# Wider multiplications on VectorE: spectra in six blocks, and three pairs of small instructions merged

## The chip, the cores and the metric

The kernel runs on one core of a Trainium2 chip. The metric is the device time of one launch in microseconds, the median of several runs. The engines of the core are TensorE (matrix products), VectorE and GpSimd (elementwise work), ScalarE (activations and copies) and SyncE, whose queue issues all DMA transfers here.

## The reference, cut to what matters

```python
def _autocorrelation(Q, K, V):              # here K = V = ctx, 8 x 512 x 2048, 8 heads
    qf = jnp.fft.fft(q, axis=2)
    kf = jnp.fft.fft(k, axis=2)
    corr = jnp.fft.ifft(qf * jnp.conj(kf), axis=2).real
    topk = int(C * np.log(L))               # 12 lags for L = 512
    w, idx = jax.lax.top_k(corr.transpose(0, 1, 3, 2), topk)
    w = jax.nn.softmax(w, axis=-1)
    out = jnp.zeros_like(v)
    for i in range(topk):                   # v shifted by each lag, clamped at the last position
        g = jnp.minimum(idx[:, :, None, :, i] + pos, L - 1)
        out = out + w[:, :, None, :, i] * jnp.take_along_axis(v, g, axis=2)
...
x = x + _autocorrelation(_layernorm(x), ctx, ctx)
out = einsum('bsd,od->bso', h, W) + bias     # h = _layernorm(x)
upd = einsum('ebsr,eor,e->bso', einsum('bsd,erd->ebsr', h, A), Bf, coeffs * scales)
x = x + out + upd
```

Each channel of x is correlated over the 512 positions with the same channel of the context. The 12 largest lags get softmax weights, and the context is summed at these shifts. A dense layer with a low-rank update follows.

## The kernel before

The batch (8) and the channels (2048, in chunks of 256) give N = 64 chunks. The program walks through 78 windows. Window w takes chunk w through the correlation and the choice of lags, chunk w - 1 through the weighted sum of shifts, and chunks w + 1 and w + 2 through preparation. From window 14 on it also holds one eighth of the dense layer's product for one half of a group of 512 output columns, so that a batch takes eight windows. Windows 1 to 9 prepare the dense weights (`p_w`, `p_hi`, `p_lo`). Rows of a finished batch (`a_rows`) get the attention added by GpSimd (`add_row`), in four windows of each eight.

All transforms are matrix products. A 512-point transform is folded into four parts of 128 frequencies. TensorE leaves a spectrum of a chunk in PSUM as two pairs of blocks, `ps[:, 2]` and `ps[:, 3]`, each 2 x 256 columns. ScalarE moves the two spectra of the context, `vk` (of the values) and `uk` (of the upper half), to SBUF (`move_spectrum`). A product of two spectra needs each PSUM pair twice, with different blocks of the moved spectrum, and a sum or difference of the results on GpSimd.

VectorE works in a fixed order in each window: `scale_group` (dense output), `multiply_queries` (4 products of 512 columns, into `prod` and `term`, which is the buffer `tf`), `multiply_upper` (4, into `zu` and `tu`), statistics, `multiply_lower` (8, into `zv`, `zf`, `tw`, `tf`), `row_low`, then for the new correlation `part_corr`, `largest`, `choose`, `weights_low`, then `row_statistics`, `part_output` and `row_gain`. `largest` finds the eight largest lags of each of the two halves g of a chunk and negates the maximum; ScalarE takes the exponentials (`exponents`, into `wts`), `choose` removes the chosen lags, sums the kept exponentials into `total`, scales it by a constant and takes the reciprocal `share`.

GpSimd's order in a window is `add_products`, `add_group` (dense output), `add_upper`, `add_lower`, `add_row`, `fold_queries`, `fold_values`, `add_bias`. TensorE's order is `upper_lags` and `lower_lags` of chunk w - 1 (from the transposed weights `w_lag`), `correlate`, `values` and `upper` of chunk w + 1, `output` of chunk w - 1, `queries` of chunk w + 1, with eight pieces of the dense product between them. SyncE's queue is in order too: in a window with a row addition it waits for it, stores the sum (`store_x1`) and loads the next attention rows before it issues the two transposes of the weights (`turn_weights`). Engines wait for each other by counting semaphores; `q_used`, `w1_used` and `w0_used` count twice for each chunk, once for each PSUM pair read.

Of the kernel before, what the change touches and what calls it, by code (L numbers as in the profile page):

```python
# [14 lines left out]
T = 128  # L35
# [3 lines left out]
CH = 256  # L39
# [192 lines left out]
def flow(nc, shared, x, W, A, Bf, coeffs, scales, parts, x1s, hrow, bias, whi, wlo, wscale, out):  # L232
# [12 lines left out]
    with ExitStack() as ctx:  # L245
# [44 lines left out]
        vk = [sb(f"a_vk{i}", [T, 5, CH]) for i in range(2)]  # L290
        uk = [sb(f"a_uk{i}", [T, 5, CH]) for i in range(2)]
        prod = sb("a_prod", [T, 4, CH])
        zu = sb("a_zu", [T, 4, CH])
        zv = sb("a_zv", [T, 4, CH])
        zf = sb("a_zf", [T, 4, CH])
        tu = sb("a_tu", [T, 4, CH])
        tw = sb("a_tw", [T, 4, CH])
        tf = sb("a_tf", [T, 4, CH])
        term = tf
        wts = sb("a_wts", [T, SUB, L])  # L300
# [621 lines left out]
        def _(act):  # L922
            def copy(out, source, **how):
                return nc.scalar.activation(out, source, ACT.Copy, **how)  # L924
# [37 lines left out]
            def move_spectrum(n, dst, mm, moved, patched):  # L962

                act.wait_ge(mm, 2 * n + 1)
                copy(dst[:, 1:3, :], ps[:, 2, :, :])
                copy(dst[:, 0, :], ps[:, 2, 0, :]).then_inc(moved, 1)
                act.wait_ge(mm, 2 * n + 2)
                copy(dst[:, 3, :], ps[:, 3, 0, :], scale=rows_but_0[:, 0:1])
                copy(dst[:, 4, :], ps[:, 3, 1, :])
                act.wait_ge(moved, n + 1)  # L970
                copy(dst[0:1, 1, :], ps[0:1, 3, 0, :]).then_inc(patched, 1)
# [22 lines left out]
            def exponents(n):  # L994

                at_least(act, kept, SUB * n)
                for g in range(SUB):
                    act.wait_ge(max_negated, SUB * n + g + 1)
                    nc.scalar.activation(wts[:, g, :], corr[:, g, :], ACT.Exp, bias=minus_max[:, g:g + 1]
                                         ).then_inc(exp_done, 1)  # L1000
# [7 lines left out]
            def scale(n):  # L1008
                at_least(act, w_turned, 2 * (n - dma_turns(n)))
                at_least(act, w_dma, 32 * dma_turns(n))  # L1010
                for g in range(SUB):
                    act.wait_ge(share_known, SUB * n + g + 1)
                    act.wait_ge(lags_folded, SUB * n + g + 1)
                    copy(w_row[:, 0, g, :], corr[:, g, :], scale=share[:, g:g + 1]).then_inc(scaled, 1)
# [95 lines left out]
        def _(pool):  # L1110
# [42 lines left out]
            def add_products(n):  # L1153
                pool.wait_ge(q_used, 2 * (n + 1))
                add(prod[:, 0:2, :], term[:, 0:2, :], ALU.add).then_inc(prod_added, 1)
                add(prod[:, 2:4, :], term[:, 2:4, :], ALU.subtract).then_inc(prod_added, 1)
# [83 lines left out]
        def _(dve):  # L1240
            def product(out, a, b):
                return nc.vector.tensor_tensor(out, a, b, ALU.mult)  # L1242

            def multiply_queries(n):
# [3 lines left out]
                at_least(dve, corr_mm, SUB * n)  # L1248
                at_least(dve, z_added, n - 1)
                dve.wait_ge(q_mm, 2 * n + 1)  # L1250
                product(prod[:, 0:2, :], ps[:, 2, :, :], v[:, 0:3:2, :])
                product(term[:, 2:4, :], ps[:, 2, :, :], v[:, 3:5, :]).then_inc(q_used, 1)
                dve.wait_ge(q_mm, 2 * n + 2)
                product(prod[:, 2:4, :], ps[:, 3, :, :], v[:, 1:3, :])
                product(term[:, 0:2, :], ps[:, 3, :, :], v[:, 3:5, :]).then_inc(q_used, 1)

            def multiply_upper(n):
# [5 lines left out]
                product(zu[:, 0:2, :], ps[:, 0, :, :], u[:, 0:3:2, :])  # L1263
                product(zu[:, 2:4, :], ps[:, 0, :, :], u[:, 3:5, :]).then_inc(w1_used, 1)
                dve.wait_ge(w1_mm, 2 * n + 2)
                product(tu[:, 0:2, :], ps[:, 1, :, :], u[:, 3:5, :])
                product(tu[:, 2:4, :], ps[:, 1, :, :], u[:, 1:3, :]).then_inc(w1_used, 1)

            def multiply_lower(n):

                u, v = uk[n % 2], vk[n % 2]
                at_least(dve, z_added, n)
                dve.wait_ge(w0_mm, 2 * n + 1)
                product(zv[:, 0:2, :], ps[:, 2, :, :], v[:, 0:3:2, :])
# [5 lines left out]
                product(tw[:, 0:2, :], ps[:, 3, :, :], v[:, 3:5, :])  # L1280
                product(tw[:, 2:4, :], ps[:, 3, :, :], v[:, 1:3, :])
                product(tf[:, 0:2, :], ps[:, 3, :, :], u[:, 3:5, :])
                product(tf[:, 2:4, :], ps[:, 3, :, :], u[:, 1:3, :]).then_inc(w0_used, 1)
# [8 lines left out]
            def largest(n):  # L1292
# [253 lines left out]
```

## Time and profile before

| what | us |
|---|---|
| median of three runs | 2646.55 |
| lowest and highest run | 2646.3, 2653.88 |
| span of the profiled execution, first to last instruction | 2644.4 |
| TensorE products busy | 2497.7 |
| GpSimd busy | 2155.5 |
| VectorE busy | 1901.7 |
| ScalarE busy | 1055.7 |

The profiled execution's time is its span plus what lies around it, which the profile does not show; two of the three runs lie 1.9 and 2.15 us above the span. Busy time is the union of an engine's instructions, so two that overlap in its pipeline count once.

### The profile page before, as it was taken

The numbers are of one execution on the slowest core, as the hardware profiler recorded it, in microseconds if no ns is written. First come the engines' busy times: TensorE is split into PE (matmuls) and PEld (weight loads), VectorE is DVE, ScalarE is ACT, GpSimd is POOL, SyncE is SP. The second block draws the span as 40 slices with busy tenths as digits, with TensorE's granted clock in tenths as the row PEclk, the third lists the DMA queues.
The fourth block names the chain that finished last, engine by engine and source line by source line (L and its number), as shares of the span: only waits on it lengthen the run. The fifth ranks groups of instructions, "written<-read, shape, count | busy, mean of one in ns | idle before, by whom it ended". The sixth has DMA issues, their size and how long they took to land.

```text
span 2644.4 us, 36606 instructions
## 1 busy us (share of the span) xinstructions
PE 2497.7 (94%) x12288; PEld 1559.9 (59%) x12288; DVE 1901.7 (72%) x4966; ACT 1055.7 (40%) x1906; POOL 2155.5 (82%) x1558
## 2 busy tenths in 40 slices
PE   4999866799999999999999999999999999999998
PEld 3655555566666656666666666666666666654444
DVE  5989989778787788777877788778876688645000
ACT  4788855533443343533443334533333233201000
POOL 5799999778998799988998899888998899654222
PEclk8999978899999999999999999999999999999999
DMA  9399998966788687966887687957786687758853
GB/s 325 99 261 269 269 244 198 231 192 209 254 266 228 219 252 238 277 203 210 258 270 210 217 275 248 271 181 236 253 250 172 219 265 243 199 203 301 268 180 114
DMA packets 550028, 613.19 MB, mean 232 GB/s; under 512 B 322640, under 2 KB 448720, under 8 KB 532176
## 3 DMA queue, kind: packets, MB, share of 16 engines
q1 hardware_dynamic: 549840, 610.86, 76.6%
q8 instruction: 97, 1.59, 0.2%
q14 instruction: 91, 0.75, 0.1%
HBM read 383.22 MB, written 151.00 MB: 202 GB/s over the span
## 4 chain that ended last, share of the span: by engine, by line
PE 53%; POOL 22%; DVE 8%; DMA 7%; SPq 5%; issue 4%; ACT 1%; POOLq 0%; DVEq 0%; ACTq 0%
PE f_ps L840 11%; PE f_ps L844 11%; PE f_ps L842 11%; PE a_ps L718 7%; PE a_ps L805 5%; PE a_ps L763 4%; POOL a_zu L1115 4%; POOL f_x1p L1115 4%; POOL a_rows L1115 3%; DMA a_w_lag<-a_w_row 2%; PE a_ps L821 2%; PE a_ps L820 2%; POOL a_zv L1115 2%; POOL a_zf L1115 2%; PE a_ps L768 1%
## 5 line engine op out<-in xcount | busy, mean ns | idle before, releaser
L840 PE MATMUL f_ps<-f_whi,f_hhi 128*128 128x512 f16 x2048 | 777.3, 380 | 5.6 <-issue 2.4
L844 PE MATMUL f_ps<-f_whi,f_hlo 128*128 128x512 f16 x2048 | 777.4, 380 | 0.0
L842 PE MATMUL f_ps<-f_wlo,f_hhi 128*128 128x512 f16 x2048 | 777.4, 380 | 0.0
L924 ACT ACTIVATE a_side<-a_ps 128x256 f32<-128x256 f32 (+1 forms) x320 | 128.0, 416 | 873.5 <-PE a_ps L805 698.4
L844 PEld LDWEIGHTS f_ps<-f_whi,f_hlo 128*128 128x128 f16 x2048 | 200.6, 98 | 242.3 <-issue 1.1
L842 PEld LDWEIGHTS f_ps<-f_wlo,f_hhi 128*128 128x128 f16 x2048 | 200.7, 98 | 230.8 <-issue 1.1
L840 PEld LDWEIGHTS f_ps<-f_whi,f_hhi 128*128 128x128 f16 x2048 | 200.7, 98 | 220.6 <-issue 6.7
L1115 POOL TENSOR_TENSOR a_prod<-a_prod,a_tf 128x512 f32<-128x512 f32 x128 | 160.2, 1273 | 138.7 <-DVE a_tf L1242 138.7
L1115 POOL TENSOR_TENSOR a_zv<-a_zv,a_tw 128x512 f32<-128x512 f32 x128 | 183.3, 1450 | 100.5 <-DVE a_tf L1242 100.5
L805 PE MATMUL a_ps<-inv,a_prod 128*128 128x256 f32 x1024 | 239.5, 388 | 25.6 <-POOL a_prod L1115 25.6
L1115 POOL TENSOR_TENSOR f_x1p<-f_x1p,f_y 128x512 f32<-128x512 f32 x128 | 172.7, 1381 | 101.0 <-DVE f_y L1242 101.0
L763 PE MATMUL a_ps<-a_w_lag,lags 128*128 128x256 f16 x1536 | 232.3, 274 | 23.0 <-DMA a_w_lag<-a_w_row 18.0
L805 PEld LDWEIGHTS a_ps<-inv,a_prod 128*128 128x128 f32 x1024 | 198.6, 195 | 65.2 <-POOL a_prod L1115 32.0
L1242 DVE TENSOR_TENSOR f_y<-f_ps,f_scale 128x512 f32<-128x512 f32 x128 | 81.0, 686 | 186.2 <-PE f_ps L844 169.5
L1115 POOL TENSOR_TENSOR f_x1p<-f_x1p,f_bias 128x2048 f32<-128x2048 f32 x32 | 147.5, 4608 | 69.8 <-DMA f_x1p<-x_scratch 69.8
L763 PEld LDWEIGHTS a_ps<-a_w_lag,lags 128*128 128x128 f16 x1536 | 149.7, 98 | 69.0 <-DMA a_w_lag<-a_w_row 23.4
L1115 POOL TENSOR_TENSOR a_zu<-a_zu,a_tu 128x512 f32<-128x512 f32 x128 | 172.3, 1367 | 5.1 <-DVE a_tu L1242 5.1
L1115 POOL TENSOR_TENSOR a_rows<-a_rows,f_attn 128x2048 f32<-128x2048 f32 x32 | 144.2, 4507 | 36.1 <-DMA f_attn<-parts_scratch 36.1
L1115 POOL TENSOR_TENSOR a_zf<-a_zf,a_tf 128x512 f32<-128x512 f32 x128 | 159.2, 1262 | 0.0
L1115 POOL TENSOR_TENSOR a_zu<-a_zu,a_zv 128x512 f32<-128x512 f32 x128 | 158.9, 1257 | 0.0
L718 PE MATMUL a_ps<-a_tv,fold 128*128 128x256 f32 x512 | 129.6, 398 | 26.8 <-ACT a_vk L924 26.8
L1026 ACT ACTIVATE a_rows<-a_rows,f_shift,f_gain 128x2048 f32<-128x2048 f32 x32 | 67.0, 2095 | 218.1 <-DVE f_shift L1384 154.9
(137 smaller groups left out, 5236.6 us busy)
## 6 DMA issues: line engine op xcount, KB each, us to landing
f_whi<-whi_scratch SPq DMA_DIRECT2D x128, 512.0 KB, 5.1
f_wlo<-wlo_scratch SPq DMA_DIRECT2D x128, 512.0 KB, 6.5
a_rows<-in_x_dram SPq DMA_DIRECT2D x62, 1024.0 KB, 8.7
vs<-in_ctx_dram SPq DMA_DIRECT2D x64, 512.0 KB, 6.2
xs<-in_x_dram SPq DMA_DIRECT2D x64, 512.0 KB, 8.0
parts_scratch<-a_so SPq DMA_DIRECT2D x64, 512.0 KB, 7.5
x_scratch<-a_rows SPq DMA_DIRECT2D x32, 1024.0 KB, 5.1
f_x1p<-x_scratch SPq DMA_DIRECT2D x32, 1024.0 KB, 6.8
```

What stands on the lines that cost most here:

```text
L718: return nc.tensor.matmul(ps[:, pair, j, :], fold[:, k, :], source, start=True, stop=True)
L763: mm = nc.tensor.matmul(out, lag_mat[:, constant, 2 * cls + k, :], w_lag[:, part, main::TB, :], start=(constant + part == 0), stop=(consta ...
L805: mm = nc.tensor.matmul(corr[:, g, cls * 2 * T:(cls + 1) * 2 * T], prod[:, 2 * k + cls, g * T:(g + 1) * T], inv[:, cls, k, :], start=(k == ...
L820: nc.tensor.matmul(ps[:, 2 + j, i, :], outm[:, k0, :], z[:, s0, :], start=True, stop=False)
L821: mm = nc.tensor.matmul(ps[:, 2 + j, i, :], outm[:, k1, :], z[:, s1, :], start=False, stop=True)
L840: nc.tensor.matmul(f_ps[:, t, :], h_hi[q][:, kq, rows_t], w_hi[u % WR][:, :, kq, :], start=(k == 0), stop=False)
L842: nc.tensor.matmul(f_ps[:, t, :], h_hi[q][:, kq, rows_t], w_lo[u % WR][:, :, kq, :], start=False, stop=False)
L844: mm = nc.tensor.matmul(f_ps[:, t, :], h_lo[q][:, kq, rows_t], w_hi[u % WR][:, :, kq, :], start=False, stop=(k == DB - 1))
L924: return nc.scalar.activation(out, source, ACT.Copy, **how)
L1026: nc.scalar.activation(rows[w % 2][:, :], rows[w % 2][:, :], ACT.Identity, bias=f_shift[:, 0:1], scale=f_gain[:, 0:1]).then_inc(h_done, 1)
L1115: return nc.gpsimd.tensor_tensor(whole, whole, part, op)
L1242: return nc.vector.tensor_tensor(out, a, b, ALU.mult)
```

## The change

Each moved spectrum gets six blocks instead of five: the first PSUM pair, then the second (its first row masked), then the first pair again with its first row replaced. Blocks 0 to 3 are then what the first PSUM pair is multiplied with, and blocks 2 to 5 what the second is multiplied with, both as 1024 contiguous columns. `vk` and `uk` of a chunk lie in one buffer `vu`, `zv` and `zf` in one (`zvf`), `tw` and `tf` in one (`twf`). VectorE reads a PSUM pair twice (or four times) in one instruction by a step of zero. `multiply_queries` and `multiply_upper` become two instructions of 1024 columns each, `multiply_lower` two of 2048. GpSimd's second subtraction of the query products takes its operands the other way round. The two negations of `largest`, the two scalings of `total` and the two reciprocals become one instruction each, which waits for both halves. `wts` shares its memory with `prod`.

```diff
-        vk = [sb(f"a_vk{i}", [T, 5, CH]) for i in range(2)]
-        uk = [sb(f"a_uk{i}", [T, 5, CH]) for i in range(2)]
+        vu = [sb(f"a_vu{i}", [T, 2, 6, CH]) for i in range(2)]
+        vk = [vu[i][:, 0, :, :] for i in range(2)]
+        uk = [vu[i][:, 1, :, :] for i in range(2)]
...
-        wts = sb("a_wts", [T, SUB, L])
+        wts = prod[:, :, :].rearrange("p (g h) c -> p g (h c)", g=SUB)
...
             def move_spectrum(n, dst, mm, moved, patched):
 
                 act.wait_ge(mm, 2 * n + 1)
-                copy(dst[:, 1:3, :], ps[:, 2, :, :])
-                copy(dst[:, 0, :], ps[:, 2, 0, :]).then_inc(moved, 1)
+                copy(dst[:, 4:6, :], ps[:, 2, :, :])
+                copy(dst[:, 0:2, :], ps[:, 2, :, :]).then_inc(moved, 1)
                 act.wait_ge(mm, 2 * n + 2)
-                copy(dst[:, 3, :], ps[:, 3, 0, :], scale=rows_but_0[:, 0:1])
-                copy(dst[:, 4, :], ps[:, 3, 1, :])
+                copy(dst[:, 2, :], ps[:, 3, 0, :], scale=rows_but_0[:, 0:1])
+                copy(dst[:, 3, :], ps[:, 3, 1, :])
                 act.wait_ge(moved, n + 1)
-                copy(dst[0:1, 1, :], ps[0:1, 3, 0, :]).then_inc(patched, 1)
+                copy(dst[0:1, 4, :], ps[0:1, 3, 0, :]).then_inc(patched, 1)
...
-                    act.wait_ge(max_negated, SUB * n + g + 1)
+                    act.wait_ge(max_negated, n + 1)
+                    act.wait_ge(corr_mm, SUB * (n + 1))
...
+            def twice_over(spectrum):
+
+                return spectrum.rearrange("p j c -> p (j c)").unsqueeze(1).broadcast_to([T, 2, 2 * CH])
+
+            def paired(blocks):
+
+                return blocks.rearrange("p (a j) c -> p a (j c)", a=2)
+
+            def four_over(spectrum):
+
+                return spectrum.rearrange("p j c -> p (j c)").unsqueeze(1).unsqueeze(1).broadcast_to([T, 2, 2, 2 * CH])
+
+            def both(blocks):
+
+                return blocks.rearrange("p b (a j) c -> p b a (j c)", a=2)
...
                 at_least(dve, corr_mm, SUB * n)
+                at_least(dve, kept, SUB * n)
                 at_least(dve, z_added, n - 1)
                 dve.wait_ge(q_mm, 2 * n + 1)
-                product(prod[:, 0:2, :], ps[:, 2, :, :], v[:, 0:3:2, :])
-                product(term[:, 2:4, :], ps[:, 2, :, :], v[:, 3:5, :]).then_inc(q_used, 1)
+                product(paired(prod[:, :, :]), twice_over(ps[:, 2, :, :]), paired(v[:, 0:4, :])).then_inc(q_used, 1)
                 dve.wait_ge(q_mm, 2 * n + 2)
-                product(prod[:, 2:4, :], ps[:, 3, :, :], v[:, 1:3, :])
-                product(term[:, 0:2, :], ps[:, 3, :, :], v[:, 3:5, :]).then_inc(q_used, 1)
+                product(paired(term), twice_over(ps[:, 3, :, :]), paired(v[:, 2:6, :])).then_inc(q_used, 1)
...
                 dve.wait_ge(w0_mm, 2 * n + 1)
-                product(zv[:, 0:2, :], ps[:, 2, :, :], v[:, 0:3:2, :])
-                product(zv[:, 2:4, :], ps[:, 2, :, :], v[:, 3:5, :])
-                product(zf[:, 0:2, :], ps[:, 2, :, :], u[:, 0:3:2, :])
-                product(zf[:, 2:4, :], ps[:, 2, :, :], u[:, 3:5, :]).then_inc(w0_used, 1)
+                product(both(zvf[:, :, :, :]), four_over(ps[:, 2, :, :]), both(vu[n % 2][:, :, 0:4, :])
+                        ).then_inc(w0_used, 1)
...
-                for g in range(SUB):
-                    dve.wait_ge(top_a_found, SUB * n + g + 1)
-                    nc.vector.tensor_scalar(minus_max[:, g:g + 1], top_a[:, g, 0:1], -1.0, None, ALU.mult
-                                            ).then_inc(max_negated, 1)
+                dve.wait_ge(top_a_found, SUB * (n + 1))
+                nc.vector.tensor_scalar(minus_max[:, :], top_a[:, :, 0], -1.0, None, ALU.mult).then_inc(max_negated, 1)
...
-                for g in range(SUB):
-                    dve.wait_ge(kept, SUB * n + g + 1)
-                    nc.vector.tensor_scalar(total[:, g:g + 1], total[:, g:g + 1], 1.0 / LAG_SCALE, None, ALU.mult
-                                            ).then_inc(total_scaled, 1)
-                for g in range(SUB):
-                    dve.wait_ge(total_scaled, SUB * n + g + 1)
-                    nc.vector.reciprocal(share[:, g:g + 1], total[:, g:g + 1]).then_inc(share_known, 1)
+                dve.wait_ge(kept, SUB * (n + 1))
+                nc.vector.tensor_scalar(total, total, 1.0 / LAG_SCALE, None, ALU.mult).then_inc(total_scaled, 1)
+                dve.wait_ge(total_scaled, n + 1)
+                nc.vector.reciprocal(share, total).then_inc(share_known, 1)
```

## Rows read from the trace of the kernel before

**Rows 1.** Three stretches: busy of each engine, granted clock, DMA share, GB/s.
```profile
core 0: us, PE busy (x) PEld busy (x) DVE busy (x) ACT busy (x) POOL busy (x), PEclk, DMA share, GB/s
175.00:210.00 35.00, 31.35 (x138) 20.39 (x137) 31.23 (x90) 28.19 (x41) 33.03 (x23) 1.00 1.00 268
...
315.00:502.00 187.00, 125.34 (x599) 96.26 (x597) 160.58 (x434) 113.51 (x187) 175.46 (x128) 0.84 0.90 225
...
587.00:2347.00 1760.00, 1741.80 (x8805) 1107.01 (x8804) 1361.50 (x3537) 662.79 (x1302) 1552.46 (x1135) 1.00 0.76 234
```

**Rows 2.** TensorE's waits, 510 to 2340 us: total us, times, longest.
```profile
PE a_ps L763 <- DMA a_w_lag<-a_w_row: 18.0, 10, 4.0
```

**Rows 3.** Timeline of TensorE: start, us, instruction [pause before it].
```profile
687.58 0.50 PE L763 MATMUL a_ps<-a_w_lag,lags 128*128 128x256 f16 x3 [3.01 <-DMA a_w_lag<-a_w_row]
...
762.53 0.50 PE L763 MATMUL a_ps<-a_w_lag,lags 128*128 128x256 f16 x3 [0.51 <-DMA a_w_lag<-a_w_row]
...
984.48 0.50 PE L763 MATMUL a_ps<-a_w_lag,lags 128*128 128x256 f16 x3 [3.97 <-DMA a_w_lag<-a_w_row]
...
1316.42 0.50 PE L763 MATMUL a_ps<-a_w_lag,lags 128*128 128x256 f16 x3 [0.32 <-DMA a_w_lag<-a_w_row]
...
2159.40 0.50 PE L763 MATMUL a_ps<-a_w_lag,lags 128*128 128x256 f16 x3 [1.40 <-DMA a_w_lag<-a_w_row]
```

**Rows 4.** Chain of waits, 575 to 780 us: start, us, what.
```profile
622.44 1.21 DVE a_tf L1242 x2
623.72 2.49 POOL a_zv L1115 x2
...
672.90 4.49 POOL a_rows L1115
...
680.70 6.84 DMA a_w_lag<-a_w_row
687.58 0.50 PE a_ps L763 x3
```

**Rows 5.** Chain of waits, early stage: start, us, what.
```profile
106.17 1.20 DVE a_tf L1242 x2
...
283.11 0.77 ACT a_vk L924 x2
...
410.51 6.02 PE a_ps L805 x16
...
425.61 0.20 DVE a_sums L1325 x2
...
475.12 1.20 DVE a_tf L1242 x2
```

**Rows 6.** Groups of VectorE by form: shapes, count, busy us, mean ns.
```profile
L1242 DVE TENSOR_TENSOR a_zv<-a_ps,a_vk 128x512 f32<-128x512 f32 x128 | 82.2, 684 | 32.2 <-PE a_ps L763 30.9
...
L1394 DVE TENSOR_TENSOR f_rowlo<-a_rows,f_ps 128x2048 f16<-128x2048 f32 x4 | 9.1, 2279 | 0.0
...
L1430 DVE TENSOR_SCALAR p_bt<-f_ps,p_mix 128x2048 f32<-128x2048 f32 x2 | 7.4, 3704 | 1.0 <-PE f_ps L859 1.0
```

**Rows 7.** Timeline of VectorE, lower products: start, us from first start to last end.
```profile
618.77 1.28 DVE L1242 TENSOR_TENSOR a_zv<-a_ps,a_vk 128x512 f32<-128x512 f32 x2
619.97 1.28 DVE L1242 TENSOR_TENSOR a_zf<-a_ps,a_uk 128x512 f32<-128x512 f32 x2
```

**Rows 8.** Timelines of VectorE and ScalarE, second maximum to exponentials.
```profile
628.44 0.69 DVE L1295 MAX8 a_top_a<-a_ps 128x8 f32<-128x512 f32 x1
629.05 0.27 DVE L1298 TENSOR_SCALAR a_minus_max<-a_top_a 128x1 f32<-128x1 f32 x2
...
629.28 1.27 ACT L999 ACTIVATE a_wts<-a_ps,a_minus_max 128x512 f32<-128x512 f32 x2 [2.17 <-DVE a_minus_max L1298]
```

**Rows 9.** Groups of ScalarE by form, copies of a spectrum.
```profile
L924 ACT ACTIVATE a_vk<-a_ps 128x256 f32<-128x256 f32 x128 | 51.5, 402 | 0.0
...
L924 ACT ACTIVATE a_vk<-a_ps 128x512 f32<-128x512 f32 x64 | 38.2, 597 | 2.6 <-PE a_ps L718 2.6
```

**Rows 10.** Stretches behind three pauses, columns as in rows 1.
```profile
688.00:692.00 4.00, 4.00 (x19) 2.37 (x18) 2.58 (x4) 2.17 (x5) 3.37 (x4) 0.57 0.96 328
...
985.00:989.00 4.00, 4.00 (x19) 2.30 (x18) 2.58 (x4) 1.08 (x3) 2.44 (x3) 0.57 1.04 334
...
1280.00:1284.00 4.00, 4.00 (x28) 2.43 (x26) 2.48 (x4) 2.53 (x5) 4.00 (x5) 1.00 0.98 325
```

More of the change, by code:

```diff
@@ L289, in flow @@
         tv = sb("a_tv", [T, TB, CH])
-        vk = [sb(f"a_vk{i}", [T, 5, CH]) for i in range(2)]
-        uk = [sb(f"a_uk{i}", [T, 5, CH]) for i in range(2)]
+        vu = [sb(f"a_vu{i}", [T, 2, 6, CH]) for i in range(2)]
+        vk = [vu[i][:, 0, :, :] for i in range(2)]
+        uk = [vu[i][:, 1, :, :] for i in range(2)]
         prod = sb("a_prod", [T, 4, CH])
         zu = sb("a_zu", [T, 4, CH])
-        zv = sb("a_zv", [T, 4, CH])
-        zf = sb("a_zf", [T, 4, CH])
+        zvf = sb("a_zvf", [T, 2, 4, CH])
+        zv, zf = zvf[:, 0, :, :], zvf[:, 1, :, :]
         tu = sb("a_tu", [T, 4, CH])
-        tw = sb("a_tw", [T, 4, CH])
-        tf = sb("a_tf", [T, 4, CH])
+        twf = sb("a_twf", [T, 2, 4, CH])
+        tw, tf = twf[:, 0, :, :], twf[:, 1, :, :]
         term = tf
-        wts = sb("a_wts", [T, SUB, L])
+        wts = prod[:, :, :].rearrange("p (g h) c -> p g (h c)", g=SUB)
         side = sb("a_side", [T, SUB, 2 * T])
@@ L1011, in scale @@
                 for g in range(SUB):
-                    act.wait_ge(share_known, SUB * n + g + 1)
+                    act.wait_ge(share_known, n + 1)
                     act.wait_ge(lags_folded, SUB * n + g + 1)
@@ L1155, in add_products @@
                 add(prod[:, 0:2, :], term[:, 0:2, :], ALU.add).then_inc(prod_added, 1)
-                add(prod[:, 2:4, :], term[:, 2:4, :], ALU.subtract).then_inc(prod_added, 1)
+                nc.gpsimd.tensor_tensor(prod[:, 2:4, :], term[:, 2:4, :], prod[:, 2:4, :], ALU.subtract
+                                        ).then_inc(prod_added, 1)
             def add_upper(n):
@@ L1262, in multiply_upper @@
                 dve.wait_ge(u_patched, n + 1)
-                product(zu[:, 0:2, :], ps[:, 0, :, :], u[:, 0:3:2, :])
-                product(zu[:, 2:4, :], ps[:, 0, :, :], u[:, 3:5, :]).then_inc(w1_used, 1)
+                product(paired(zu[:, :, :]), twice_over(ps[:, 0, :, :]), paired(u[:, 0:4, :])).then_inc(w1_used, 1)
                 dve.wait_ge(w1_mm, 2 * n + 2)
-                product(tu[:, 0:2, :], ps[:, 1, :, :], u[:, 3:5, :])
-                product(tu[:, 2:4, :], ps[:, 1, :, :], u[:, 1:3, :]).then_inc(w1_used, 1)
+                product(paired(tu[:, :, :]), twice_over(ps[:, 1, :, :]), paired(u[:, 2:6, :])).then_inc(w1_used, 1)
             def multiply_lower(n):
-                u, v = uk[n % 2], vk[n % 2]
                 at_least(dve, z_added, n)
                 dve.wait_ge(w0_mm, 2 * n + 1)
-                product(zv[:, 0:2, :], ps[:, 2, :, :], v[:, 0:3:2, :])
-                product(zv[:, 2:4, :], ps[:, 2, :, :], v[:, 3:5, :])
-                product(zf[:, 0:2, :], ps[:, 2, :, :], u[:, 0:3:2, :])
-                product(zf[:, 2:4, :], ps[:, 2, :, :], u[:, 3:5, :]).then_inc(w0_used, 1)
+                product(both(zvf[:, :, :, :]), four_over(ps[:, 2, :, :]), both(vu[n % 2][:, :, 0:4, :])
+                        ).then_inc(w0_used, 1)
                 dve.wait_ge(w0_mm, 2 * n + 2)
                 dve.wait_ge(prod_added, 2 * min(n + 2, N))
[L1280 to L1283, printed above, removed]
+                product(both(twf[:, :, :, :]), four_over(ps[:, 3, :, :]), both(vu[n % 2][:, :, 2:6, :])
+                        ).then_inc(w0_used, 1)
             def part_corr(n):
```

## The prediction

> **What bounds the kernel.** I read the stretches by engine first, then TensorE's waits, then the chain of waits, and last the single instructions the change touches. Between 587 and 2347 us [rows 1] TensorE is busy 1741.80 of 1760 us at granted clock 1.00. In this stage VectorE is busy 1361.50 us, so it has room, and making it cheaper is worth nothing by itself. What can be won there are TensorE's pauses, and the list of its waits has one entry only: ten waits for the transposed weights `a_w_lag`, 18.0 us together [rows 2]. So this stage can give 18 us and what hangs on the pauses, however much VectorE saves.
>
> The pauses are not alike [rows 3]: six are first in their batch (1.40 to 3.97 us; the shortest, a middle one and the longest are shown), four are second ones of 0.32 to 0.53 us. The chain of waits says how a first one comes about [rows 4]. VectorE's products of chunk n end at 623.65, GpSimd starts `a_zv` at 623.72 and from there works without a break through two windows, which hold two row additions and one output group, SyncE may issue the transposes only behind the store that waits for the second row addition, and `a_w_lag` lands near 687.5. Every link hangs on the end of those products. Products that end earlier move the whole run, and TensorE's pause at 687.58 shrinks by as much, until it is gone.
>
> The early stage is another matter. Up to 502 us no engine is full. At 175 to 210 us the 16 DMA engines are at 1.00, and at 315 to 502 us the granted clock is 0.84 [rows 1]. The chain there changes hands among VectorE, ScalarE, GpSimd and DMA. The products are on it in seven episodes, whose `a_tf` ends lie at 107 to 476 us (first and last in [rows 5]).
>
> The last stage, behind 2347 us, holds no product of a spectrum, so I count it as zero.
>
> **The change, step by step.** *Products.* A 512-column product lasts 684 ns [rows 6], but four in a row start 0.60 us apart: the `a_zv` pair starts at 618.77, the `a_zf` pair at 619.97 [rows 7]. So part of the 684 ns overlaps with the next instruction, and what a removed instruction saves is its pitch less its columns. The columns cost (2279 - 684) / 1536 = 1.04 ns each, from the 2048-column instruction that also reads PSUM [rows 6], so 0.53 us for 512; a removed start saves 0.60 - 0.53 = 0.067 us. Four products become two for the queries (0.13 us), four become two for the upper half (0.13), eight become two for the lower half (0.40): 0.67 us for each chunk. The estimate for the new instructions is 684 + 512 x 1.04 = 1.22 us for 1024 columns and 2.28 us for 2048. All consumers wait for the second count of each product semaphore, or run behind it, so nothing that used the first half early loses by this.
>
> Against this stands a rule of the Trainium skill, VectorE: DVE Perf Modes, The DRAIN you can't avoid: the next VectorE instruction is held until the pipeline has emptied, so that the number of instructions is what counts. The same page's section on the TRN2 errata gives (N + 151) / 0.96 ns for such an operation, that is 157 ns for each instruction removed, and 1.57 us for a chunk instead of 0.67. Its 691 ns for 512 columns agree with the row's 684, but the pitch of 0.60 us in the rows contradicts a full wait between two instructions, and I go by the rows.
>
> *Broadcast reads.* No row of before has VectorE read one PSUM block twice in one instruction. Below nothing it can't go much, since each product still takes its columns; I take no extra cost, by the 2279 ns row, which it is nearest to: inner runs of 512 contiguous columns from PSUM. The upper bound is the instruction with an awkward pattern, 3704 ns for the same 2048 columns [rows 6], 0.70 ns more a column.
>
> *One negation for two.* The second maximum runs 628.44 to 629.13, the first negation starts at 629.05 and the exponential follows at 629.28 [rows 8]. The joint negation can't start before 629.13 plus its 0.14 us, so the first exponential starts about 0.1 us later (bounds 0 to 0.2), and the replacement that waits for it too. That is a loss.
>
> *Totals and reciprocals.* The two reciprocals of a chunk take 0.20 us of the chain at 425.61 [rows 5]. One instruction in place of two saves a start, but now each waits for the other's end, where the two halves covered each other. I take zero (bounds 0.2 gain, 0.1 loss).
>
> *ScalarE's copies.* One copy of each spectrum grows from 256 to 512 columns, 402 to 597 ns [rows 9]: 0.2 us more, twice a chunk. ScalarE is idle for more than half of the span (busy 662.79 of 1760 us [rows 1]), so it costs nothing in the steady stage, except where the chain runs through it. In the early chain it does (the two `a_vk` copies at 283.11 [rows 5]): TensorE's next product waits for them. The exponentials now write into `a_prod`; the products that overwrite it come later on VectorE than the sums that read the exponentials, so that wait is met. GpSimd's subtraction keeps its size.
>
> **The sum.** *Steady stage, first pauses:* six, each shorter by 0.67 us: 4.0 us. *Second pauses:* three follow the same way from the lower products alone, 0.40 us each, but not more than the pause itself (0.51, 0.53, 0.35): 1.15 us. The one at 1316.42 hangs on the maximum, the exponential and ScalarE's copies instead, and grows by about 0.3 us. Net 0.85 us. *Clock:* behind the pauses of 3.01 and 3.97 us the next 4 us have a granted clock of 0.57, that is a part at 1.2 GHz instead of 2.4; behind 2.69 us it stays at 1.00 [rows 10]. Each such spell loses 4 x 0.43 = 1.7 us. The first pause becomes 2.34 us, and I let its spell vanish; the second becomes 3.30 us, and I let it stay: 1.7 us. Together 6.55 us.
>
> *Early stage:* five episodes hold all products (0.67 each), two only the upper and lower ones (0.53): 4.4 us. On the same chain the negation stands four times (0.4), the `a_vk` copies three times (0.6) and the `a_uk` copies once (0.2): 1.2 us given back. Net 3.2 us (bounds 0 to 4.4).
>
> Sum 9.75 us. The profiled execution's span is 2644.4 us; the median of the runs, 2646.55, lies 2.15 us above it, for what is outside the span, and I let that stay: 2646.55 - 9.75 = 2636.8, rounded to 2637.
>
> **Rivals.** *(a) The early gain is absorbed and the clock spell stays.* For it: DMA at 1.00 in the stretch 175 to 210 [rows 1]; a transfer that starts 0.6 us earlier into a full set of engines doesn't land earlier. Against: the chain has the DMA waits between episodes, not beside them. Then 1 us early and 4.85 us steady: 2641, with 2640 to 2645 as its span. *(b) Each removed instruction gives 0.157 us.* A removed start would have to be worth the whole overhead, no overlap; the pitch of 0.60 us speaks against. It is what the Trainium skill's page on VectorE above gives. Then 6 x 1.57 = 9.4, second pauses 1.1, both spells 3.4, early 5 x 1.57 + 2 x 1.31 - 1.2 = 9.3: 23 us, 2623. *(c) Slower: the doubled PSUM read costs more by the column.* With 0.70 ns more on the 8192 product columns of a chunk, each chunk's products grow by 5.7 - 0.67 = 5 us; six GpSimd runs start 5 us later (30 us), five early episodes grow by 5 us and two, without the queries, by 3.8 (33 us): 2710. It decides from 0.67 / 8192 = 0.08 ns a column on. Against it: the inner runs are contiguous. *(d) The early clock.* At 315 to 502 us TensorE's matmuls on the chain run in part at half clock: 16 of `a_ps` take 6.02 us at 410.51 [rows 5]. A shift of 0.5 us may put one or two such pieces at either level, 3 us each: 2631 to 2643 around the likeliest.
>
> **How the numbers follow.** Sum as worked out 0.45 (its own range 2633 to 2641); (a) 0.30; (d) on the good side 0.08; nothing visible, 2645 to 2648, 0.06; (b) 0.04; (c) or (d) on the bad side, slower, 0.07. The range 2630 to 2646 leaves out (b), the slower cases and part of no change, under 2 in 10. About 0.3%, 8 us, is what a measurement of this kernel tells from no change, so faster means below 2638.6: about 0.8 of the first case with (b) and the good side of (d), 0.48. Within 0.3%: 0.45. Slower: 0.07.
>
> **What would show it.** Product instructions of about 1.22 and 2.28 us, 384 of them for spectra instead of 1024, and 0.6 to 0.7 us less between the first product of a chunk and its last where VectorE is not kept waiting. First pauses for `a_w_lag` near 2.3, 3.3 and 0.7 us where 3.01, 3.97 and 1.40 stand; the ten waits together near 13 us. No fall of the clock behind the first. The first exponential 0.1 us later behind its maximum. Wrong would be: products of 2048 columns above 2.4 us (then (c)); pauses shorter by more than 1 us (then (b), or GpSimd's run has another start); unchanged pauses with earlier products, which would mean that the DMA, not GpSimd's run, sets the landing.

## The result and the profile after

The changed kernel takes 2914.59 us, the median of four runs (2908.21 to 2918.61), against 2646.43 us before, also the median of four (2639.78 to 2653.88). The ratio is 1.101, with an interval of 1.099 to 1.103. The forecast was 2637 us with a range to 2646; the kernel became 268 us slower.

The page of the kernel after: busy time by engine, and the chain that ended last by line.

```profile
PE 2584.4 (89%) x12288; PEld 1595.9 (55%) x12288; DVE 2202.7 (76%) x4134; ACT 1081.5 (37%) x1906; POOL 2155.2 (74%) x1558
...
PE f_ps L821 11%; PE f_ps L823 11%; PE f_ps L825 11%; DVE a_minus_max L1288 9%; PE a_ps L699 8%; PE a_ps L786 6%; PE a_ps L744 5%; PE a_ps L801 3%; PE a_ps L802 3%; ACT a_vu L905 2%; PE a_ps L749 2%; DVE a_top_a L1286 1%; ACT a_prod L981 1%; DMA x_scratch<-a_rows 1%; SPq L537 1%
```

VectorE has 832 instructions fewer than before (4134 against 4966) and is busy 301 us longer (2202.7 against 1901.7). Nine per cent of the chain is one line, the negation of the maximum (L1288 here, L1298 before). The same groups of VectorE by form (line, shapes, count, busy us, mean ns):

```profile
L1288 DVE TENSOR_SCALAR a_minus_max<-a_top_a 128x2 f32<-128x2 f32 x64 | 289.4, 4523 | 2.2
L1225 DVE TENSOR_TENSOR a_zvf<-a_ps,a_vu 128x2048 f32<-128x2048 f32 x64 | 146.3, 2286 | 33.1 <-PE a_ps L744 32.9 <-issue 0.2
...
L1309 DVE TENSOR_SCALAR a_sums<-a_sums 128x2 f32<-128x2 f32 x64 | 85.4, 1335 | 2.2
L1225 DVE TENSOR_TENSOR a_prod<-a_ps,a_vu 128x1024 f32<-128x1024 f32 x64 | 78.2, 1222 | 82.0 <-PE a_ps L699 81.6 <-issue 0.3
L1311 DVE RECIPROCAL a_sums<-a_sums 128x2 f32<-128x2 f32 x64 | 10.6, 166 | 2.2
```

The wide products, which answer to the first line of [rows 6], last what was forecast. Two numbers on each of 128 partitions, negated, take 4.52 us on average; before, one negation of one column took 0.145 us (128 of them, 17.4 us). The scaling of the totals takes 1.34 us where one column took 0.152. The joint reciprocal, which is as small, takes 0.17 us. The negation before, by form, then its instructions by themselves (shortest, median and longest in ns; first and last start in us):

```profile
L1298 DVE TENSOR_SCALAR a_minus_max<-a_top_a 128x1 f32<-128x1 f32 x128 | 17.4, 145 | 0.0
...
L1298 DVE TENSOR_SCALAR a_minus_max<-a_top_a x128: 129/148/155, 42.6 to 2322.8; 128x1 f32<-128x1 f32 x128
```

The instructions of L1288, after, in the same way:

```profile
L1288 DVE TENSOR_SCALAR a_minus_max<-a_top_a x64: 238/4314/11969, 42.0 to 2583.1; 128x2 f32<-128x2 f32 x64
```

An instruction with the same two columns that lasts from 0.24 to 11.97 us doesn't compute for that time; something holds it. What holds it is seen where one of them meets the other engines. The timelines of the kernel after, of VectorE, GpSimd, ScalarE and TensorE, merged in order of start (start, us from start to end, instruction, [idle before]):

```profile
1013.51 0.70 DVE L1286 MAX8 a_top_a<-a_ps 128x8 f32<-128x512 f32 x1
1013.71 2.47 POOL L1097 TENSOR_TENSOR a_zu<-a_zu,a_zvf 128x512 f32<-128x512 f32 x2
1014.24 8.87 DVE L1288 TENSOR_SCALAR a_minus_max<-a_top_a 128x2 f32<-128x2 f32 x1
1016.15 4.49 POOL L1097 TENSOR_TENSOR a_rows<-a_rows,f_attn 128x2048 f32<-128x2048 f32 x1
1020.61 1.25 POOL L1126 TENSOR_TENSOR a_tq<-xs 128x512 f32<-128x512 f32 x1
1021.83 1.25 POOL L1127 TENSOR_TENSOR a_tq<-xs 128x512 f32<-128x512 f32 x1
1023.16 1.26 POOL L1131 TENSOR_TENSOR xs<-a_tq 128x512 f32<-128x512 f32 x1
1023.19 1.27 ACT L981 ACTIVATE a_prod<-a_ps,a_minus_max 128x512 f32<-128x512 f32 x2 [11.02 <-DVE a_minus_max L1288]
1024.35 1.08 ACT L905 ACTIVATE a_vu<-a_ps 128x512 f32<-128x512 f32 x2
1025.49 2.07 PE L699 MATMUL a_ps<-a_tv,fold 128*128 128x256 f32 x4 [6.83 <-ACT a_vu L905]
```

GpSimd's additions each start about 0.03 us before the one ahead has ended, so there is no gap between them, up to the first instruction that waits for GpSimd's own result: the `xs` addition reads the `a_tq` that ends at 1021.83 + 1.25 = 1023.08 and starts at 1023.16. In this gap of 0.08 us the negation ends (1014.24 + 8.87 = 1023.11). Then the exponentials run, ScalarE's copies of the next spectrum stand behind them in its queue, and TensorE, which needs these copies for `upper`, has stood still for 6.83 us.

Not every hold ends in such a gap. All 64 negations of this execution start while GpSimd is in an instruction. The 60 that last above 0.4 us end 0.02 to 0.04 us behind the end of one of its instructions, 57 of them after one to seven others have ended. For 28 of the 60 GpSimd then stands still; for 32 its next addition had already started, as here:

```profile
1146.24 3.32 DVE L1288 TENSOR_SCALAR a_minus_max<-a_top_a 128x2 f32<-128x2 f32 x1
1148.82 0.71 POOL L1097 TENSOR_TENSOR a_zvf<-a_zvf,last 1x256 f32<-1x256 f32 x1
1149.50 2.48 POOL L1097 TENSOR_TENSOR a_zu<-a_zu,a_zvf 128x512 f32<-128x512 f32 x2
```

This negation ends at 1149.56, the addition of one row at 1149.53, and the next one started at 1149.50. None of the 60 lasts through a gap. So a gap lets the negation in, but it isn't needed; what decides which addition's end does so stays open.

Behind TensorE's pause of 6.83 us the clock is low (columns as in [rows 1], the granted clock, 0.58, behind the engines' busy times):

```profile
1025.00:1029.00 4.00, 3.51 (x10) 2.71 (x11) 3.89 (x14) 3.18 (x9) 0.65 (x1) 0.58 0.57 236
```

The waits of the kernel after (total us, times, longest):

```profile
ACT a_prod L981 <- DVE a_minus_max L1288: 398.6, 54, 14.1
...
PE a_ps L699 <- ACT a_vu L905: 221.2, 61, 10.9
```

and the second of them before:

```profile
PE a_ps L718 <- ACT a_vk L924: 26.8, 13, 5.7
```

TensorE's wait for the copied spectrum was 26.8 us over the span of before; now it is 221.2. The wait for transposed weights, the whole of [rows 2], has fallen to 5.1 us: what was to be won has been covered by something larger. The account over the span: TensorE idle 2910.4 - 2584.4 = 326.0 us against 2644.4 - 2497.7 = 146.7, that is 179.3 us more; busy for 86.7 us longer with the same 12288 matmuls, at a mean granted clock of 0.947 instead of 0.984. Together 266 us, the difference of the spans.

### The profile page after: what moved, and what is told of

Read it like the earlier page. It is cut to its first block, busy times and chain, and to the rows that moved or that the text cites. A ratio compares the mean times of both kernels' runs of the same rounds, so it can differ in the third digit from the quotient of the medians.

```text
span 2910.4 us, 35840 instructions
## 1 busy us (share of the span) xinstructions
PE 2584.4 (89%) x12288; PEld 1595.9 (55%) x12288; DVE 2202.7 (76%) x4134; ACT 1081.5 (37%) x1906; POOL 2155.2 (74%) x1558
## 4 chain that ended last, share of the span: by engine, by line
PE 60%; DVE 13%; ACT 4%; issue 2%; DMA 2%; SPq 1%; POOL 1%; ACTq 0%; POOLq 0%; DVEq 0%
PE f_ps L821 11%; PE f_ps L823 11%; PE f_ps L825 11%; DVE a_minus_max L1288 9%; PE a_ps L699 8%; PE a_ps L786 6%; PE a_ps L744 5%; PE a_ps L801 3%; PE a_ps L802 3%; ACT a_vu L905 2%; PE a_ps L749 2%; DVE a_top_a L1286 1%; ACT a_prod L981 1%; DMA x_scratch<-a_rows 1%; SPq L537 1%
## 5 line engine op out<-in xcount | busy, mean ns | idle before, releaser
L1097 POOL TENSOR_TENSOR a_zvf<-a_zvf,a_twf 128x512 f32<-128x512 f32 x256 | 339.9, 1357 | 121.6 <-DVE a_twf L1225 121.6
L699 PE MATMUL a_ps<-a_tv,fold 128*128 128x256 f32 x512 | 186.9, 528 | 221.2 <-ACT a_vu L905 221.2
L1288 DVE TENSOR_SCALAR a_minus_max<-a_top_a 128x2 f32<-128x2 f32 x64 | 289.4, 4523 | 2.2
L1097 POOL TENSOR_TENSOR a_prod<-a_prod,a_twf 128x512 f32<-128x512 f32 x64 | 81.6, 1275 | 273.4 <-DVE a_twf L1225 273.4
L699 PEld LDWEIGHTS a_ps<-a_tv,fold 128*128 128x128 f32 x512 | 124.8, 259 | 279.0 <-ACT a_vu L905 254.5
L1097 POOL TENSOR_TENSOR f_x1p<-f_x1p,f_y 128x512 f32<-128x512 f32 x128 | 160.5, 1288 | 108.5 <-DVE f_y L1225 108.5
L981 ACT ACTIVATE a_prod<-a_ps,a_minus_max 128x512 f32<-128x512 f32 x128 | 81.0, 684 | 426.2 <-DVE a_minus_max L1288 398.6
L1225 DVE TENSOR_TENSOR a_twf<-a_ps,a_vu 128x1024 f32<-128x1024 f32 (+1 forms) x128 | 223.6, 1747 | 0.8 <-PE a_ps L699 0.7
L905 ACT ACTIVATE a_vu<-a_ps 128x512 f32<-128x512 f32 (+2 forms) x512 | 217.2, 484 | 17.0 <-PE a_ps L699 16.7
L1097 POOL TENSOR_TENSOR a_zu<-a_zu,a_tu 128x512 f32<-128x512 f32 x128 | 184.8, 1468 | 4.8 <-DVE a_tu L1225 4.8
```

What stands on the lines that cost most here:

```text
L699: return nc.tensor.matmul(ps[:, pair, j, :], fold[:, k, :], source, start=True, stop=True)
L1097: return nc.gpsimd.tensor_tensor(whole, whole, part, op)
L1288: nc.vector.tensor_scalar(minus_max[:, :], top_a[:, :, 0], -1.0, None, ALU.mult).then_inc(max_negated, 1)
```

## The experiments

The theory was that the two-column scalings, not the wide products, cost the 268 us, because GpSimd's unbroken runs hold them. The rival was that the products read doubled PSUM blocks at a price that shows in other instructions, and that the long negation is only where the loss is booked. The runs of before beside the first four experiments have a median of 2651.01 us (11 runs), those beside the last four 2648.33 us (26 runs).

**The products alone.** The changed kernel with the three pairs of small instructions taken apart again:

```diff
...
-                dve.wait_ge(top_a_found, SUB * (n + 1))
-                nc.vector.tensor_scalar(minus_max[:, :], top_a[:, :, 0], -1.0, None, ALU.mult).then_inc(max_negated, 1)
+                for g in range(SUB):
+                    dve.wait_ge(top_a_found, SUB * n + g + 1)
+                    nc.vector.tensor_scalar(minus_max[:, g:g + 1], top_a[:, g, 0:1], -1.0, None, ALU.mult
+                                            ).then_inc(max_negated, 1)
...
-                dve.wait_ge(kept, SUB * (n + 1))
-                nc.vector.tensor_scalar(total, total, 1.0 / LAG_SCALE, None, ALU.mult).then_inc(total_scaled, 1)
-                dve.wait_ge(total_scaled, n + 1)
-                nc.vector.reciprocal(share, total).then_inc(share_known, 1)
+                for g in range(SUB):
+                    dve.wait_ge(kept, SUB * n + g + 1)
+                    nc.vector.tensor_scalar(total[:, g:g + 1], total[:, g:g + 1], 1.0 / LAG_SCALE, None, ALU.mult
+                                            ).then_inc(total_scaled, 1)
...
+                    nc.vector.reciprocal(share[:, g:g + 1], total[:, g:g + 1]).then_inc(share_known, 1)
```

> The changed kernel with its three small pairs taken apart again: wide products, six-block spectra and shared buffers stay. Theory (the joint two-column scalings on VectorE are held up while GpSimd works): negations back to 0.15 us each, and the time is what the forecast gave for the wide products alone, 2630 to 2646 us. Rival (the wide products with their doubled PSUM reads, or the longer copies on ScalarE, make the loss): near 2900 us. A mixed outcome, 2650 to 2850, would mean that both share it.

Measured: 2671.39 us (six runs), ratio 1.0076, interval 1.0061 to 1.0091. So nearly the whole loss is gone with the three pairs, and the rival with it; but what is left is a loss too, where a gain of 10 us was forecast. The products last 1223, 1215 and 2286 ns. What is new is in `row_low`, which subtracts two SBUF operands. Its instructions in this kernel (shortest, median, longest ns):

```profile
L1385 DVE TENSOR_TENSOR f_rowlo<-a_rows,f_rowhi x28: 2281/2762/13065, 654.1 to 2483.2; 128x2048 f16<-128x2048 f32 x28
```

Before, the same line reads

```profile
L1394 DVE TENSOR_TENSOR f_rowlo<-a_rows,f_rowhi x28: 2281/2328/5586, 658.4 to 2458.9; 128x2048 f16<-128x2048 f32 x28
```

Three of them, at 1357.66, 1661.7 and 2256.6 us, last 13.06 us. The first in the timelines of VectorE and GpSimd with the products alone:

```profile
1355.46 2.28 DVE L1225 TENSOR_TENSOR a_twf<-a_ps,a_vu 128x2048 f32<-128x2048 f32 x1
1357.38 0.72 POOL L1097 TENSOR_TENSOR a_zu<-a_zu,last 1x256 f32<-1x256 f32 x1
1357.66 13.06 DVE L1385 TENSOR_TENSOR f_rowlo<-a_rows,f_rowhi 128x2048 f16<-128x2048 f32 x1
1358.07 4.93 POOL L1097 TENSOR_TENSOR a_zvf<-a_zvf,a_twf 128x512 f32<-128x512 f32 x4
...
1367.32 1.25 POOL L1127 TENSOR_TENSOR a_tq<-xs 128x512 f32<-128x512 f32 x1
1368.65 3.20 POOL L1131 TENSOR_TENSOR xs<-a_tq 128x512 f32<-128x512 f32 x1
```

and the same place in the kernel before:

```profile
1361.81 1.28 DVE L1242 TENSOR_TENSOR a_tf<-a_ps,a_uk 128x512 f32<-128x512 f32 x2
1362.24 0.72 POOL L1115 TENSOR_TENSOR a_zu<-a_zu,last 1x256 f32<-1x256 f32 x1
1363.00 2.28 DVE L1394 TENSOR_TENSOR f_rowlo<-a_rows,f_rowhi 128x2048 f16<-128x2048 f32 x1
1363.17 4.47 POOL L1115 TENSOR_TENSOR a_zv<-a_zv,a_tw 128x512 f32<-128x512 f32 x2 [0.21 <-DVE a_tf L1242]
```

Before, GpSimd's small addition ended at 1362.96 and GpSimd then stood idle for 0.21 us, waiting for the last product; `f_rowlo` came at 1363.00, into that idle time, and was through in 2.28 us. With the wide products the last product ends earlier against GpSimd's order: `f_rowlo` comes at 1357.66, 0.44 us before the small addition ends (1358.10), GpSimd finds its next operand ready, goes on without a gap, and `f_rowlo` waits until the gap behind 1367.32 + 1.25 = 1368.57. There it runs for about its usual time, and now GpSimd's `xs` addition is the one that waits (3.20 us instead of 1.26). In TensorE's waits between 510 and 2360 us this gives the line that [rows 2] didn't have:

```profile
PE a_ps L699 <- ACT a_vu L905: 18.5, 3, 6.2
PE a_ps L744 <- DMA a_w_lag<-a_w_row: 16.8, 8, 3.6
```

**The negation alone, the totals alone.** The kernel before with the joint negation only, and with the joint scaling and reciprocal only:

```diff
...
+                dve.wait_ge(top_a_found, SUB * (n + 1))
+                nc.vector.tensor_scalar(minus_max[:, :], top_a[:, :, 0], -1.0, None, ALU.mult).then_inc(max_negated, 1)
```

> The kernel before with one change: the two negations of the maxima become one instruction of two columns. Theory: it lasts 3 to 5 us instead of 0.3 us for two, since it is held until GpSimd's run of instructions has a break, and the time is 2860 to 2930 us, nearly the whole loss. Rival (products): 2646 us, within 0.3%. Rival (it is the wait for both maxima or the strided read that costs, not GpSimd): the instruction is long by a fixed amount, the same in each window, whatever GpSimd does.

```diff
...
+                dve.wait_ge(kept, SUB * (n + 1))
+                nc.vector.tensor_scalar(total, total, 1.0 / LAG_SCALE, None, ALU.mult).then_inc(total_scaled, 1)
+                dve.wait_ge(total_scaled, n + 1)
+                nc.vector.reciprocal(share, total).then_inc(share_known, 1)
```

> The kernel before with one change: the two scalings of the totals and the two reciprocals become one instruction each, of two contiguous columns. Theory: the scaling is held like the negation (1 to 4 us, by where GpSimd stands), the reciprocal is not (0.17 us); ScalarE's copies of a spectrum don't wait for it, so much of it is hidden: 2650 to 2750 us. Rival (strided read or the wait for two maxima is at fault): 0.15 us for the scaling and 2646 us.

Measured: 2856.77 us for the negation alone (ratio 1.077, 1.075 to 1.079), just under the 2860 that was the lower end of the theory, and 2737.04 for the totals alone (1.033, 1.031 to 1.034), inside it. The negation alone, by form:

```profile
L1297 DVE TENSOR_SCALAR a_minus_max<-a_top_a 128x2 f32<-128x2 f32 x64 | 267.5, 4180 | 2.2
```

The totals alone, by form:

```profile
L1320 DVE TENSOR_SCALAR a_sums<-a_sums 128x2 f32<-128x2 f32 x64 | 193.2, 3019 | 2.2
L1322 DVE RECIPROCAL a_sums<-a_sums 128x2 f32<-128x2 f32 x64 | 10.6, 166 | 2.2
```

Each is held without any wide product in the kernel. The negations last from 0.25 to 10.11 us, so this is no fixed price of the strided read, and the scaling, whose two columns are contiguous, is held too. The parts don't add up: 7.7 and 3.3 and 0.8 per cent are 11.8, and together they cost 10.1. In the changed kernel a total is held for 1.34 us, alone for 3.02. It fits that an instruction behind one that has already waited for GpSimd finds less of GpSimd's run ahead of it; no run shows it by itself.

**Gaps in GpSimd's run.** The changed kernel, with two waits of GpSimd for its own results around the last addition of `add_lower`:

```diff
...
-                add(zu[:, 0:2, :], zv[:, 0:2, :], ALU.add)
+                add(zu[:, 0:2, :], zv[:, 0:2, :], ALU.add).then_inc(zu_half, 1)
+                pool.wait_ge(zu_half, n + 1)
                 add(zu[:, 2:4, :], zv[:, 2:4, :], ALU.add).then_inc(z_added, 1)
+                pool.wait_ge(z_added, n + 1)
```

> The changed kernel as it is, but GpSimd waits for its own previous addition twice within its run (between the two last additions of zu, and behind them), which puts two breaks of about 0.1 us where it had none. Theory (the held instruction gets in only where GpSimd's run breaks): the negation's mean falls from 4.5 us to 1.5 to 2.5 us, and the time from 2915 to 2700 to 2800 us, though GpSimd itself gets slower by 0.2 us a window. Rival (the hold has a fixed length, or lasts as long as GpSimd is active at all): 4.5 us and 2915 us or more.

Measured: 2687.0 us, ratio 1.014 (1.0126 to 1.0155), a little below the 2700 to 2800 of the theory. GpSimd does the same work, VectorE the same instructions, and the loss falls from 10.1 to 1.4 per cent. By form:

```profile
L1291 DVE TENSOR_SCALAR a_minus_max<-a_top_a 128x2 f32<-128x2 f32 x64 | 110.2, 1722 | 2.2
L1312 DVE TENSOR_SCALAR a_sums<-a_sums 128x2 f32<-128x2 f32 x64 | 55.5, 868 | 2.2
```

That is the strongest evidence that GpSimd's run holds the two: with gaps of its own making most of the loss is gone. But the negation doesn't get in only where the run breaks, as the theory had it. Of the 61 negations above 0.4 us in this run, 27 end in one of the new gaps, one in an old one, and 33 behind an addition whose successor had already started. How much of the cure is the gaps themselves, and how much that the negations now meet GpSimd's order at other places, is not separated.

**Three columns.** Is it that the number of columns is even, so that the work can be split into halves? A single run of the changed kernel with a third, unused column in the negation (its input is set to zero once):

```diff
-        top_a = sb("a_top_a", [T, SUB, 8])
+        top_a = sb("a_top_a", [T, SUB + 1, 8])
...
-        minus_max = sb("a_minus_max", [T, SUB])
+        minus_max = sb("a_minus_max", [T, SUB + 1])
...
+            nc.vector.memset(top_a[:, :, :], 0.0)
```

> The changed kernel, but the joint negation takes three columns instead of two (the third is a spare that is set once and never used). Theory (the instruction is held because its columns are split in two streams, the second of which shares with GpSimd; the split needs no even number, only the same number on both sides): still held, a mean of 3 to 5 us, near 2915 us. Rival (only an even number of columns is split): 0.15 us, and a time of 2670 to 2740 us, since the totals still have two.

Measured: 2907.91 us. By form:

```profile
L1288 DVE TENSOR_SCALAR a_minus_max<-a_top_a 128x3 f32<-128x3 f32 x64 | 285.1, 4455 | 2.2
```

Three are held as two are. An odd number is no way out when source and target have the same one.

**The products alone, with a gap ahead of `add_lower`.** One line in GpSimd's order, so that `f_rowlo` finds a gap whichever side is early; and the kernel before with the same line, as the control:

```diff
             def add_lower(n):
 
+                pool.wait_ge(zu_raised, n + 1)
                 pool.wait_ge(w0_used, 2 * (n + 1))
```

> The kernel with the wide products and the small pairs apart, and one line more: GpSimd waits for its own small addition to zu before it starts add_lower. Theory (in the run before, VectorE's subtraction f_rowlo, which reads two SBUF buffers, came while GpSimd was still busy, found no break and was held 13.06 us in three windows; the faster products brought it there early): the break of about 0.1 us lets it in, no f_rowlo lasts over 4 us, TensorE's three pauses of 6.2 us for ScalarE's copies are gone, and the time is what the forecast gave for the products, 2636 to 2648 us. Rival (the three holds are a coincidence of GpSimd's place and stay): three holds of 13 us, 2670 us. Rival (the longer copies on ScalarE or the doubled reads cost the rest): no hold, but still over 2655 us.

> The kernel before with the same one line in GpSimd and nothing else, to see what the break is worth by itself. Theory: none of its f_rowlo was held over 3.5 us in the steady stage, so the break costs about 0.1 us a window where GpSimd is on the path and gives nothing: 2646 to 2651 us, within 0.3%. Rival (the break helps the kernel before as much): 2636 us.

Measured: 2642.87 us for the products with the gap (eight runs, 2634.39 to 2645.5; ratio to before 0.9973, 0.996 to 0.9985) and 2654.24 for the kernel before with the gap (twelve runs, 2646.56 to 2658.71; 1.0021, 1.001 to 1.0032). The two sets of runs don't overlap. So the gap costs the kernel before 5.9 us, more than the theory allowed (2651 us at most), and the wide products, in the same GpSimd order, are worth 11.4 us. Against the kernel before without the gap, products and gap together are worth 5.5 us (2648.33 - 2642.87). TensorE's waits from 510 to 2340 us, with the products and the gap:

```profile
PE a_ps L744 <- DMA a_w_lag<-a_w_row: 17.0, 10, 3.8
```

and three of its pauses in the timeline of TensorE:

```profile
682.11 0.50 PE L744 MATMUL a_ps<-a_w_lag,lags 128*128 128x256 f16 x3 [2.15 <-DMA a_w_lag<-a_w_row]
...
978.56 0.50 PE L744 MATMUL a_ps<-a_w_lag,lags 128*128 128x256 f16 x3 [3.79 <-DMA a_w_lag<-a_w_row]
...
1273.24 0.50 PE L744 MATMUL a_ps<-a_w_lag,lags 128*128 128x256 f16 x3 [2.05 <-DMA a_w_lag<-a_w_row]
```

The same two views of the control:

```profile
PE a_ps L763 <- DMA a_w_lag<-a_w_row: 23.6, 11, 5.2
```

```profile
689.86 0.82 PE L763 MATMUL a_ps<-a_w_lag,lags 128*128 128x256 f16 x3 [3.95 <-DMA a_w_lag<-a_w_row]
...
986.71 0.75 PE L763 MATMUL a_ps<-a_w_lag,lags 128*128 128x256 f16 x3 [4.31 <-DMA a_w_lag<-a_w_row]
...
1282.74 0.50 PE L763 MATMUL a_ps<-a_w_lag,lags 128*128 128x256 f16 x3 [3.47 <-DMA a_w_lag<-a_w_row]
```

With products and gap the line for `a_vu` is gone, and no `f_rowlo` between 510 and 2340 us lasts above 3.3 us. The control has one that comes ahead of the gap and is held:

```profile
1034.96 6.43 DVE L1395 TENSOR_TENSOR f_rowlo<-a_rows,f_rowhi 128x2048 f16<-128x2048 f32 x1
```

What this hold costs the control, no run shows. The six first pauses sum to 15.80 us with the wide products and to 21.40 in the control, 0.93 us less each (in the kernel before to 16.34); all waits for the weights to 6.6 us less than in the control.

**The negation on ScalarE.** The wide products, the gap, and one joint negation, but on the engine that reads it next; totals and reciprocals apart:

```diff
                 at_least(act, kept, SUB * n)
+                act.wait_ge(top_a_found, SUB * (n + 1))
+                copy(minus_max[:, :], top_a[:, :, 0], scale=-1.0).then_inc(max_negated, 1)
```

> The kernel with wide products, totals and reciprocals apart, the break in GpSimd, and the two negations as one instruction on ScalarE, which doesn't share what VectorE shares with GpSimd. Theory: 0.2 us on ScalarE, never held; first exponential about 0.15 us later than with two negations on VectorE; VectorE saves 0.3 us a window: within 0.2% of the run with the negations apart, 2636 to 2648 us. Rival (any joint negation costs, because the exponentials wait for both maxima): some 10 us above that run or more.

Measured: 2641.89 us (eleven runs), ratio 0.9973 (0.9961 to 0.9984). The joint negation among ScalarE's groups by form:

```profile
L905 ACT ACTIVATE a_minus_max<-a_top_a 128x2 f32<-128x2 f32 x64 | 13.1, 205 | 126.3 <-DVE a_top_a L1289 126.3
```

The only wait of TensorE between 510 and 2340 us:

```profile
PE a_ps L744 <- DMA a_w_lag<-a_w_row: 15.0, 6, 4.0
```

The same two columns take 205 ns on ScalarE and are never held. This kernel and the one with the products and the gap are equal within their intervals, and both are faster than the kernel before and the changed one.

## Why the prediction was wrong

**The steps that failed** are "One negation for two" ("about 0.1 us later (bounds 0 to 0.2)") and "Totals and reciprocals" ("zero (bounds 0.2 gain, 0.1 loss)"). Measured are 4.52 us for the joint negation, which by itself cost 206 us, and 1.34 us for the joint scaling, which with the joint reciprocal cost 86 by itself (2737.04 - 2651.01); the reciprocal is not held. I costed both as if only the number of starts changed. The merged form wasn't the old one with one column more: it is held while GpSimd works, and the negation stands between the maximum and the exponentials, with ScalarE's copies queued behind and TensorE's `upper` behind these. Its busy time grew by 289.4 - 17.4 = 272 us. That this is near the 266 us of the span is chance: alone, its busy time grew by 250 us (267.5 - 17.4) and cost 206 (2856.77 - 2651.01). The upper bound was the failure in method: before, no scaling from SBUF to SBUF has more than one column, so no row showed the new form, and I bounded it by its own one-column row. A nearer row was there. `f_rowlo` reads SBUF alone too, and its group before spreads from 2281 to 5586 ns with one and the same shape (to 3.45 us in the steady stage). I went by means, where the spread was the sign.

**What held it.** The Trainium skill, SBUF — State Buffer, Who interferes with whom, says that VectorE's second pair of SBUF ports is shared with GpSimd as an exclusive lock: a scaling that uses both pairs contends with GpSimd, an instruction with two SBUF inputs with a GpSimd instruction that reads SBUF, and whoever issues first has the pair for the whole instruction, while the other blocks fully. VectorE: DVE Perf Modes, Mode 2×_2P — use both read ports for one tensor, gives the condition: one source, SBUF to SBUF, an outermost dimension that is even, or odd and equal on both sides. What is held here agrees: two columns (4523 ns) and three (4455 ns) and `f_rowlo` (13065 ns), not one column (145 ns, the longest 155) or the products that read PSUM (2286 ns). Where the traces go beyond it is the length: by that rule the wait would be for one GpSimd instruction, 1.25 to 4.49 us in the timeline above, but the negation waited through five of them (two `a_zu`, `a_rows`, two `a_tq`), for 8.87 us, until GpSimd paused, and others waited through several and were then let in without a pause. That ports are the reason is the Trainium skill's account; the runs show which forms are held, that the holds end where an instruction of GpSimd ends, and that a gap ends them, but not why one end lets VectorE in and another doesn't.

**The products.** Right in mechanism. 1222 and 2286 ns were forecast as 1.22 and 2.28 us, and the doubled read costs nothing, which disposes of rival (c): it had the sign right for a wrong reason. The lower products run from 613.91 to 618.38 us with the gap, 4.47 us, where they ran from 618.77 to 623.64 [rows 7], 4.87: the 0.40 us of the forecast. Rival (b), 0.157 us for each instruction removed, would have made that 0.94.

**The pauses.** The forecast was 0.67 us off each first one. Against the control 0.93 us is measured, but against the kernel before only 0.09 (16.34 to 15.80 us for the six), so the size of this term is not shown. The early stage: the last early `f_rowlo` starts at 472.7 us with products and gap, 477.2 in the control and 476.2 before, so 4.5 or 3.5 us earlier where 3.2 was forecast. Against the control these two add up to 10.1 us. They are read from one execution of each kernel, and these two spans (2641.4 and 2656.7) lie 15.3 us apart, more than the 11.4 of the medians. The clock adds to the difference: it is low behind five of the six first pauses in the control and behind three with the products, which by the 4 us behind each loses 8.0 and 5.2 us (an estimate). The sum was 9.75.

**The clock.** The spell that was to vanish did not. Behind the pause of 2.15 us the granted clock is still 0.62 with products and gap:

```profile
683.00:687.00 4.00, 4.00 (x18) 2.20 (x17) 2.45 (x2) 2.08 (x5) 3.69 (x4) 0.62 0.99 327
```

The 1.00 behind a longer pause of before [rows 10] was no rule. So 1.7 us of the 9.75 had no ground.

**The step that was missing.** That VectorE "has room, and making it cheaper is worth nothing by itself" left out that it can be worth less than nothing. VectorE arriving 0.5 us earlier off the chain moved `f_rowlo` from GpSimd's idle 0.21 us into its run, and 10 us forecast as gain became 20 us of loss. That this collision is the whole difference between the products without and with the gap (1.0076 and 0.9973 of before, 27 us) is shown by its cure, not instruction by instruction: 18.5 us of it are TensorE's pauses for `a_vu`. In the 4.28, 4.21 and 6.32 us behind these the granted clock is 0.55, 0.58 and 0.52, which loses some 6.7 us more (an estimate); what is left stays open.

**Two slips that change no result.** The 1.31 us of rival (b) for an episode without the queries should be 1.26 (8 starts of 0.157); its 23 us stay. And GpSimd's run "without a break" behind [rows 4] has gaps of some 0.09 us where GpSimd waits for its own result, one of them up to 638.80.

## What to carry to other kernels

Before small instructions are merged, look at what shape they become and which engine works beside them at that moment: a merged instruction on the chain can cost more than all the starts it saves, and one column at a time, or ScalarE, may be the cheaper form. Read the shortest and longest time of a group, not its mean alone; a spread at one shape can be contention, and then its ends coincide with the ends of the other engine's instructions. When an engine off the chain gets faster, check by how many hundredths of a microsecond its next instruction now meets a neighbour, and if it does, one wait that makes the neighbour pause can repair it; where there was little to repair, this wait cost 5.9 us here.

## What was not expected of the hardware

A two-column scaling of VectorE from SBUF to SBUF was held for up to 11.97 us, a subtraction of two SBUF operands for 13.06 us, both through several GpSimd additions in a row; a gap of 0.08 us between two of these was enough to let VectorE in, and behind one such gap GpSimd's next addition took 3.20 us instead of 1.26. Yet 32 of the 60 longer holds of the negation ended without a gap, 0.02 to 0.04 us behind the end of an addition whose successor had already started. A two-column reciprocal (166 ns), one-column scalings (145 ns) and ScalarE's two-column copy (205 ns) beside the same GpSimd work were not held. One PSUM pair read twice or four times in one instruction cost no more than contiguous columns (1222 ns for 1024, 2286 for 2048).
